# Making the product A21·T11 one tick ahead in the chunked delta-rule attention of a decoder layer

## The reference

```python
mixed = silu(causal_conv4(x @ w_qkv)); q, k, v = split(mixed)
z = x @ w_z; beta = sigmoid(x @ w_b); g = -exp(A_log) * softplus(x @ w_a + dt_bias)
q = l2norm(q) * 128 ** -0.5; k = l2norm(k)
for t in range(128):
    S = S * exp(g[t]); delta = (v[t] - k[t] @ S) * beta[t]
    S = S + outer(k[t], delta); o[t] = q[t] @ S
og = o * silu(z); out = (og * rsqrt(mean(og ** 2) + eps) * norm_w) @ w_out
```

## Time and profile before

| | |
|---|---|
| median of 3 runs | 2256.65 us (2255.46 to 2256.8) |
| profiled execution, first to last instruction | 2253.2 us |
| TensorE, VectorE, ScalarE, GpSimd busy | 2091.6, 1711.3, 1512.7, 904.1 us |
| `k k^T` of unit 8 starts at | 167.35 us |
| `k k^T` of unit 63 starts at | 1509.89 us |

### The profile page before, as it was taken

The page is one execution under the profiler, slowest core; times in us unless marked ns, Lnnn a source line. Parts: engine busy times, 40 slices in busy tenths (PEclk is TensorE's granted clock), DMA queues, the critical chain, the costliest instruction groups (busy, mean ns, idle before and its releaser), DMA issues.

```text
span 2253.2 us, 49295 instructions
## 1 busy us (share of the span) xinstructions
PE 2091.6 (93%) x18636; PEld 1716.1 (76%) x18636; DVE 1711.3 (76%) x2944; ACT 1512.7 (67%) x3585; POOL 904.1 (40%) x714
## 2 busy tenths in 40 slices
PE   4659999999999999999999999999988899999998
PEld 4448888888888888888888888887776476666776
DVE  6789797887879788787977978787325777767665
ACT  4547777777777777777777677775767666565632
POOL 1534454444445445445535534532333123213232
PEclk8779999999999999999999999998999999999999
DMA  3432322322232332233233222212243012322232
GB/s 77 94 73 48 89 44 72 63 64 67 55 85 46 72 75 49 68 60 80 52 70 72 48 70 56 75 34 56 58 137 133 1 66 76 104 94 73 91 136 85
DMA packets 274633, 161.56 MB, mean 72 GB/s; under 512 B 209352, under 2 KB 246752, under 8 KB 269280
## 3 DMA queue, kind: packets, MB, share of 16 engines
q1 hardware_dynamic: 274400, 158.41, 27.6%
HBM read 122.43 MB, written 35.91 MB: 70 GB/s over the span
## 4 chain that ended last, share of the span: by engine, by line
issue 36%; POOL 26%; PE 23%; DVE 8%; ACT 4%; DMA 2%; SPq 2%; POOLq 0%; DVEq 0%; ACTq 0%
POOL SM L577 5%; POOL EB L493 5%; POOL Q L555 5%; PE ps L1739 4%; POOL SZ L579 3%; PE ps L1347 3%; POOL EB L497 3%; PE ps L1349 3%; PE ps L1348 3%; POOL WL L471 2%; POOL SM L585 2%; PE ps L1660 1%; ACT SC L856 1%; PE ps L1651 1%; PE ps L1480 1%
## 5 line engine op out<-in xcount | busy, mean ns | idle before, releaser
L909 DVE SCALAR_TENSOR_TENSOR A<-ps,CW,A 128x508 f32<-128x508 f32 (+2 forms) x768 | 515.9, 734 | 55.3 <-ACT A L671 50.1
L572 POOL TENSOR_SCALAR SM<-SM 128x8 f32<-128x8 f32 x64 | 12.6, 196 | 813.8 <-ACT DL L690 813.8
L1480 PE MATMUL ps<-WO,DL 128*128 128x256 f32 x1008 | 244.5, 394 | 39.5 <-POOL WO L484 24.5
L1480 PEld LDWEIGHTS ps<-WO,DL 128*128 128x128 f32 x1008 | 189.7, 194 | 74.5 <-POOL WO L484 26.4
L1347 PE MATMUL ps<-XH,WH 128*128 128x512 f32 x512 | 221.5, 433 | 26.7 <-DVE A L909 25.8
L1127 DVE TENSOR_TENSOR SZ<-SZ,ps 128x512 f32<-128x512 f32 x128 | 87.7, 687 | 201.5 <-PE ps L1514 201.4
L1349 PE MATMUL ps<-XH,WL 128*128 128x512 f32 x512 | 206.4, 403 | 0.0
L1348 PE MATMUL ps<-XL,WH 128*128 128x512 f32 x512 | 205.2, 401 | 0.0
L690 ACT ACTIVATE DL<-SZ 128x128 f32<-128x128 f32 x512 | 152.4, 298 | 38.5 <-PE ps L1514 28.8
L856 ACT ACTIVATE SC<-ps,A 128x128 f32<-128x128 f32 x512 | 141.7, 386 | 51.5 <-DVE A L1252 50.7
L1112 DVE TENSOR_TENSOR BP<-ps,EB 128x512 f32<-128x512 f32 x256 | 158.3, 681 | 3.3 <-ACT EB L665 3.3
(11 more groups left out here) (225 smaller groups left out, 5556.1 us busy)
## 6 DMA issues: line engine op xcount, KB each, us to landing
EB<-decay_rows SPq DMA_DIRECT2D x128, 256.0 KB, 4.7
WE<-expert_halves SPq DMA_DIRECT2D x32, 1024.0 KB, 5.1
x_blocks<-BP SPq DMA_DIRECT2D x256, 32.0 KB, 1.7
X<-x_blocks SPq DMA_DIRECT2D x16, 512.0 KB, 6.5
tt_blocks<-TI SPq DMA_DIRECT2D x16, 512.0 KB, 2.6
tn_blocks<-TM SPq DMA_DIRECT2D x16, 512.0 KB, 2.6
TTF<-tt_blocks SPq DMA_DIRECT2D x256, 32.0 KB, 1.9
expert_halves<-BP SPq DMA_DIRECT2D x8, 1024.0 KB, 5.8
```

Of the source, the lines that this page charges most:

```text
L909: dve.scalar_tensor_tensor(acc, ps(i, 0, [[128, 4], [1, 128 - s]]), at(CW, tile * 4 + 3 - s, [[1, 1]]), acc, ALU.mult, ALU.add).then_inc(s ...
L1480: t = pe.matmul(ps(7 - i, b * 256, [[1, 256]]), at(on_buf(k), (4 * i + 2 * b + v) * 128, [[1, 128]]), at(WO, v * 256, [[1, 256]]), start=( ...
```

## The change

Unit vn = m + 1 = n-8 now passes L1533 to L1568 one tick ahead of the unit m = n-9 whose deltas are made, and z, deltas, outputs and output projection of every unit come one tick later than before (`LAG3` 9, `LAG4` 10); v stays one unit ahead of m. All eight u2 of unit vn and all eight tt128 of unit m now stand in one alternating run of 16 products behind `k k^T`; the two separate groups, one ahead of `k k^T` and one behind on_tr, are gone. ScalarE copies u2 of a unit in one instruction of 64 x 512 in place of two of 64 x 256, and the copy of tt128 moves from behind the second on_T copy to ahead of the first. TTF is doubled, BP gets a tenth slot (made room for by a smaller DMA scratch), `EARLY` is 8, and what goes with m, k or vn modulo 4 moves by one tick against n: scale_wo and load_wo to n % 4 = 2, the split of z to n % 4 = 0, the split of v to n % 4 = 3. The pairs of decay exponentials on ScalarE move from odd to even ticks. The inverse, its copy to TM and its stores stay in the same ticks n (wn = n-7). NT is 74 in place of 73.

```diff
-LAG3, LAG4 = 8, 9
-EARLY = 7
-SLOTS = 9
+LAG3, LAG4 = 9, 10
+EARLY = 8
+SLOTS = 10
...
-        TTF = sb("TTF", 8, 128)
+        TTF = sb("TTF", 2, 8, 128)
...
+                    vn, wn = m + 1, m + 2
-                    if 0 <= vn < NSTEP and vn % 4 == 0:
-                        store_t(vn // 4)
-                    if 0 <= vn < NSTEP:
-                        load_ta(vn)
-                        load_tt(vn)
+                    if 0 <= wn < NSTEP and wn % 4 == 0:
+                        store_t(wn // 4)
+                    if 0 <= wn < NSTEP:
+                        load_ta(wn)
+                        load_tt(wn)
...
-                def u2_copy(m, i):
-                    act.wait_ge(sem["u2"], 2 * m + 1 + i)
-                    act.activation(at(U2, i * 256, [[1, 256]], 64, 64), ps(7, i * 256, [[1, 256]], 64, 64), ACT.Copy,
+                def u2_copy(n):
+                    act.wait_ge(sem["u2"], n + 1)
+                    if n:
+                        act.wait_ge(sem["tt128"], n)
+                    act.activation(at(U2, 0, [[1, 512]], 64, 64), ps(7, 0, [[1, 512]], 64, 64), ACT.Copy,
...
-                    if s3 and s1:
-                        u2_copy(m, 0)
+                    if sv:
+                        u2_copy(vn)
                     if s3:
-                        u2_copy(m, 1)
+                        act.wait_ge(sem["tt128"], m + 1)
+                        act.activation(tt(m, 64, [[128, 8], [1, 64]], 0, 64), ps(6, 0, [[64, 8], [1, 64]], 0, 64),
+                                       ACT.Copy).then_inc(sem["tt128_sb"], 1)
...
-                    if EARLY <= n and n % 2 and n + 1 < NSTEP:
+                    if EARLY <= n and n % 2 == 0 and n + 1 < NSTEP:
                         decay_exp(n + 1)
...
-                    if s3:
-                        pe.wait_ge(sem["t64_sb"], m + 1)
-                        pe.wait_ge(sem["tt64_sb"], 2 * m + 2)
-                        for pr in range(4):
-                            t = pe.matmul(ps(7, pr * 64, [[1, 64]], 64, 64), slot(m, pr * 256 + 64, [[1, 64]], 0, 64),
-                                          at(TA, pr * 64, [[1, 64]], 0, 64), start=True, stop=True)
-                        t.then_inc(sem["u2"], 1)
...
+                    if sv:
+                        pe.wait_ge(sem["t64_sb"], vn + 1)
+                        pe.wait_ge(sem["tt64_sb"], 2 * vn + 2)
                     if s3:
-                        pe.wait_ge(sem["u2_sb"], 2 * m + 1)
...
+                        pe.wait_ge(sem["u2_sb"], m + 1)
+                    for pr in pr8:
+                        if s3:
+                            t = tt128(m, pr)
+                            if pr == 7:
+                                t.then_inc(sem["tt128"], 1)
+                        if sv:
+                            t = u2(vn, pr)
+                            if pr == 7:
+                                t.then_inc(sem["u2"], 1)
```

More of the change, by code:

```diff
@@ L217, in kq_buf @@
         def kq_buf(n):
-            return A2 if n < 6 and n % 2 else A1
+            return A2 if n < 8 and n % 2 else A1
         def z_half(m, i):
@@ L651, in kq_tap3 @@
                 def kq_tap3(n):
-                    back = n - 2 if n < 6 else n - 1
+                    back = n - 2 if n <= 8 else n - 1
                     if back >= 0:
@@ L808, in _ @@
                         on_T(k, 1)
[L809 to L812, removed]
-                    if EARLY <= n and n % 2 and n + 1 < NSTEP:
+                    if EARLY <= n and n % 2 == 0 and n + 1 < NSTEP:
                         decay_exp(n + 1)
-                        decay_exp(n + 2)
+                        if n + 2 < NSTEP:
+                            decay_exp(n + 2)
                     if sv:
@@ L1041, in norm_apply @@
                                       ALU.mult).then_inc(done, 1)
-                dve.memset(at(TTF, 0, full), 0.0)
+                dve.memset(at(TTF, 0, [[1, 2048]]), 0.0)
                 dve.memset(at(TA, 0, [[1, 512]]), 0.0).then_inc(sem["zeros"], 1)
@@ L1485, in tt128, with u2 @@
                     return pe.matmul(ps(6, pr * 64, [[1, 64]], 0, 64), at(U2, pr * 64, [[1, 64]], 64, 64),
-                                     at(TTF, pr * 128 + 64, [[1, 64]], 64, 64), start=True, stop=True)
+                                     tt(m, pr * 128 + 64, [[1, 64]], 64, 64), start=True, stop=True)
+                def u2(n, pr):
+                    return pe.matmul(ps(7, pr * 64, [[1, 64]], 64, 64), slot(n, pr * 256 + 64, [[1, 64]], 0, 64),
+                                     at(TA, pr * 64, [[1, 64]], 0, 64), start=True, stop=True)
                 def deltas(m, i):
@@ L1497, in deltas @@
                         pr = 4 * i + j
-                        t = pe.matmul(ps(4 + i, j * 128, [[1, 128]]), at(TTF, pr * 128, [[1, 128]]), at(VV, pr * 128, [[1, 128]]),
+                        t = pe.matmul(ps(4 + i, j * 128, [[1, 128]]), tt(m, pr * 128, [[1, 128]]), at(VV, pr * 128, [[1, 128]]),
                                       start=True, stop=True)
@@ L1559, in _ @@
                         norms_tr(n // 4 - 1)
-                    if sv and s1:
+                    if sv:
                         v_proj(vn, 1)
@@ L1586, in _ @@
                                 t.then_inc(sem["kq_mm"], 1)
+                    if sv:
+                        pe.wait_ge(sem["t64_sb"], vn + 1)
+                        pe.wait_ge(sem["tt64_sb"], 2 * vn + 2)
                     if s3:
-                        pe.wait_ge(sem["u2_sb"], 2 * m + 1)
-                        for pr in range(4):
-                            t = pe.matmul(ps(7, (4 + pr) * 64, [[1, 64]], 64, 64), slot(m, (4 + pr) * 256 + 64, [[1, 64]], 0, 64),
-                                          at(TA, (4 + pr) * 64, [[1, 64]], 0, 64), start=True, stop=True)
-                            if pr == 3:
+                        pe.wait_ge(sem["u2_sb"], m + 1)
[4 more added lines that the diff above has]
+                                t.then_inc(sem["tt128"], 1)
+                        if sv:
+                            t = u2(vn, pr)
+                            if pr == 7:
                                 t.then_inc(sem["u2"], 1)
-                            tt128(m, pr)
                     if s4 and k < NSTEP - 1:
@@ L1598, in _ @@
                         on_tr(k, 1)
-                    if s3:
-                        pe.wait_ge(sem["u2_sb"], 2 * m + 2)
-                        for pr in range(4, 8):
-                            t = tt128(m, pr)
-                        t.then_inc(sem["tt128"], 1)
                     if s4 and k < NSTEP - 2:
```

97 lines of the change are left out of this document (45 added, 52 removed).

## The result

The changed kernel takes 2243.62 us (median of 4 runs, 2239.18 to 2245.47) against 2256.06 us (4 runs) for the kernel before: a ratio of 0.9938, 95% interval 0.9924 to 0.9952, so 12.4 us less where 9.8 were forecast. The profiled execution has a span of 2243.7 us and a time of 2245.47 us, the slowest of the four; against the span before it is 9.5 us shorter.

What follows compares the result with a forecast made beforehand. TensorE's queue and its waits ahead of out_proj were taken as the bound. Terms -17.1 - 2.8 + 0 + 16 - 3.9 - 2 made -9.8 us: 2246.8 on the median (2243.4 profiled), range 2230 to 2264.

Steps and rivals of the forecast that it cites:

- TensorE's own work: Full tick on TensorE: small groups removed and products alternated save 0.99 us a tick by its queue alone.
- What ScalarE gives of it: Two copies ahead of on_T start out_proj 1.88 us after on_tr, not 1.63; +0.02 a normal tick, taken as zero.
- signs of being wrong: Wait for L682 ahead of out_proj under 0.8 or over 1.2 us, or L486 still ending a wait.
- Ticks with the copy to TM: The 14 ticks n % 4 = 3: out_proj half 1 4.28 us after on_tr; -0.20 us each, -2.8 us.
- The scaling: GpSimd's scaling of output weights, now in n % 4 = 2, ready 0.6 us early: 13 waits go, -17.1 us.
- The start: v_proj of unit 0 stands behind products waiting for TA and TTF, delaying the first z_proj: +16 us (+12 to +18).
- The full tick that became a tail tick: m = 55 runs in tick 64 without kq: 20.0 us in place of 23.9, so -3.9 us.
- The last tick: u2 is already done between on_tr and deltas: -2 us (bounds 0 and -3).
- A: Rival: ScalarE's chain ahead of out_proj is longer than summed, +0.3 us a tick: 2265 us; chance 0.14.
- C: Rival: ScalarE's chain is shorter, -0.15 us a tick: 2237 us, at the extreme 2184; chance 0.14.
- B: Rival: the scaling is late in its new tick too, so the 17.1 us come back: 2264 us; chance 0.08.
- D: Rival: idling lowers TensorE's clock, about 6.3 us a drop, one in every four ticks: 2335 us; chance 0.03.

Runs made afterwards that it cites:

- the run with all edits: Changed kernel with the tt128 copy behind on_T, the copy to TM last, the scaling ahead of the squares and v of unit 0 early: 2202.05 us.
- the unmoved kernel: Kernel before with the scaling ahead of the squares, the copy to TM behind that of tt128, and the exponentials in even ticks: 2224.86 us.
- the moved one: Changed kernel with the copy of tt128 behind both on_T copies and the copy to TM behind that: 2203.82 us.

## Why the prediction was right

**The bound and the place** were right: TensorE's queue, with its one wait ahead of out_proj.

**TensorE's own work.** The run of sixteen was forecast at about 1.07 us and takes 1.08. One term is missing from the sum: `k k^T` takes 1.82 us (784.60 to 786.42) where behind the small group it took 1.93 (799.20 to 801.13 in the kernel before), so TensorE saves some 0.1 us more than forecast.

**What ScalarE gives of it.** out_proj was forecast 1.88 us behind on_tr and starts at 1.91; a plain tick was forecast unchanged and is 0.03 to 0.06 us shorter (the 0.1 us of `k k^T` less the later start). The idle shows as 0.81 and not 1.0, since the profile counts it from the end of on_tr's last record and the forecast from the start of the next possible matmul; the starts are what agree. The forecast named as signs of being wrong a wait under 0.8 us and any wait still ended by L486; the profile has 0.81, and its list names L486 twelve times. The starts and ends of the instructions settle both in the forecast's favour. That it is the copies' order was argued then and is shown by the run that puts one of them back: 0.49 us per plain tick return. The rule of the Trainium skill (TensorEngine Tiling (Array Packing), Performance Considerations) that emptying PSUM can become the bottleneck agrees with these rows; but what bound was the place of one 0.59 us copy in the queue, not ScalarE's capacity, for it is 67% busy.

**Ticks with the copy to TM.** -0.20 was forecast and -0.32 measured (24.88 to 24.56). Half 1 starts 4.25 us behind on_tr (4.28 forecast). The part not foreseen is the parity: with the exponentials back in that tick it takes 24.79, so 0.23 of the 0.32 us come from their move, and only 0.09 are left for what the forecast summed. That this term came out near its forecast is in part luck.

**The scaling.** -17.1 us was forecast; tick 1 went from 25.25 to 23.83, 1.42 in 13 ticks, 18.5 us. It is ready 0.46 us ahead of its user (0.6 forecast). The run with this alone gains 8 of the 12 us. The forecast did not see that in the kernel before the exponentials would have kept 0.47 us of it in each of these ticks.

**The start.** +16 was forecast, +17.6 is measured at z_proj of unit 0. A further +3.3 us in the tick of unit 0 was missed: no on_tr and no out_proj stand between the small products and deltas there, so the copy of tt128 is bare (1.35 us), then kq_proj waits 2.33 us, and the granted clock over the 9 us from 189 is 0.81, so part of them at 1.2 GHz. No run isolates these causes: the same stretch is 22.5 us in place of 24.06 in the run with the tt128 copy late and in the one not in turn, and in the kernel before the even exponentials alone bring it from 20.81 to 22.45. The window:

```profile
189.00:198.00 9.00, 6.67 (x33) 5.48 (x32) 8.93 (x11) 3.18 (x5) 0.00 (x0) 0.81 0.44 87
```

**The full tick that became a tail tick** was mis-sized: -3.9 forecast, -2.0 measured. The full tick that goes is the one of unit 63's `k k^T`, which has no kq_proj any more and took 22.4 us, not 23.9. **The tail** was taken as unchanged and grew by 1.8 us: with the copies of u2 and tt128 and splits of weights ahead of on_T in ScalarE's queue, out_proj waits 2.37 and 2.89 us where it waited 1.31 with 0.90, and 1.84. **The last tick** gave 2.5 us, 2 were forecast.

Together: 17.6 + 3.3 - 27.1 - 2.0 + 1.8 - 2.5 - 0.6 = -9.5 us of span, and the forecast -9.8: the sum is closer than its terms, and that is luck. Some 7.5 us missed at the start (4.9) and behind the full ticks (2.6) are paid by 7.2 us more in the full ticks, of which 1.7 are one tick of 26.95 us that the profiled execution before had and for which no cause was found.

**The rivals.** A and C (ScalarE's chain longer or shorter) came out between: 0.03 us longer than summed. B (the scaling late again) is refuted by tick 34's rows, though the list of waits names it; in the run with all edits the scaling ends 2.9 us ahead of out_proj and tick 2 is no shorter for it. D (the clock) is refuted in the full ticks: with 0.8 us idle in each, the granted clock stays 1.00, here and over the whole stretch from 200 to 1480 us:

```profile
760.00:784.00 24.00, 23.19 (x250) 20.29 (x250) 23.81 (x30) 14.95 (x40) 12.23 (x9) 1.00 0.23 60
```

**What the product's move is worth** is not what the change measured. With all orders mended the unmoved kernel takes 2224.86 us and the moved one 2203.82: 21 us, or 23 by the ratios. Their profiled spans, 2227.4 and 2203.0 us, differ by 24.4: from unit 1 to unit 55 the moved one takes 30.2 us less (0.50 to 0.55 in each full tick of the table), up to z_proj of unit 1 it takes 17.4 more, and behind z_proj of unit 55 it takes 11.6 less. So the full ticks and the start alone would give 13 us. The last part is the tail and what follows it; nobody had summed it, and why it is that large is not shown. In the change as it was made, ScalarE held nearly all of what the full ticks could gain, and most of the gain there (18.5 of 27.1 us) is the scaling's: k % 4 had moved by one tick against everything else.

## What to carry to other kernels

When products are moved to be faster, look next at the copies that empty them and at what else their engine must do before the next product starts: here one copy of 0.59 us in the wrong place cost 0.49 us in every plain tick. A shift of a pipeline stage by one tick also shifts every job that is done in one tick of four, and that may be worth more than what the change is about; it can be had by itself. A list of waits names one releaser for each wait: where an instruction has several, compare the ends of all of them with its start before believing it, and when a removed wait gives less than its length, look which engine has become late in that same tick.

## What the runs showed of the hardware

A 64 x 64 float32 product costs almost nothing beside one in another quarter of the array: 32 records took 1.83 us one kind after the other and 1.08 us in turn. TensorE's granted clock stayed at 1.00, 2.4 GHz, with an idle of 0.8 us in each tick of 23.8. ScalarE's copy from PSUM of 64 partitions by 512 took 0.59 us, and that of 128 by 512 took 0.58: half the partitions saved nothing.
